# ScalarE applies the instance norm straight from PSUM, and the mask and conv2 convolutions use plain weights for both images at once

## The chip, the cores and the metric

The kernel runs on one core of one Trainium2 chip. The metric is the device time of one execution in microseconds; the median of the timed runs counts. Most executions of a kernel agree within 0.3%, but the three runs of this one before the change spread by 1.4%.

## What is computed

The input x has 8 images of 32 channels and 32x32 pixels, in float32. Two blocks follow each other. The first is a transformer-like block (layer norm over rows, q, k, v by 1x1 and 3x3 convolutions, attention over the channels of a head, a gated convolution block). The change is in the second one:

```python
out = conv2d(x, conv1_w, conv1_b, 1)
mu  = jnp.mean(out, axis=(2, 3), keepdims=True)
var = jnp.var(out, axis=(2, 3), keepdims=True)
out = (out - mu) * jax.lax.rsqrt(var + EPS)
out = jnp.where(out >= 0, out, NEG_SLOPE * out)          # 0.2
# _refine(out)
out1 = conv2d(out, conv2_w, conv2_b, 1)
mask = jax.nn.sigmoid(conv2d(out, mask_w, mask_b, 1))
xm   = out * mask
q, k, v = 1x1 convolutions of xm (k and v of the padded xm)
sims = [jnp.sum(q * k[3x3 neighbour], axis=1) ...]
attn = softmax over the 9 neighbours
out2 = sum of attn * v[neighbour]
result = x + out1 * mask + (1.0 - mask) * out2
```

## The kernel before

The images are worked on in four pairs. A tile of 128 partitions holds four row blocks of 8 rows with 32 channels each, and its free size is 2 images x 256 pixels. A 3x3 convolution reads "planes": for each of the three horizontal shifts 32 partitions that hold the padded image, so that one matmul with 96 rows of weights does a whole row of taps, and three matmuls (dy) accumulate the rest. `sh_ln1`, `sh_ln2`, `sh_x2` and `sh_in` are such planes. They are filled by copies: VectorE writes shift 0 and most of shift 1 (`shift_copies`, L278, seven copies), ScalarE writes the last block of shift 1 and shift 2 (L467, five copies).

The order of each engine's instructions is written out by hand in a function `step` for each engine, and semaphores ("signals") tie the engines together. One step works on three or four pairs at once: the window part of `pair`, the gate part of `pair + 1`, the qk, v and attention part of `pair + 2`, and the first layer norm of `pair + 3`. Pairs 0 and 1 are full steps (step 0 is the body of a loop that runs once, step 1 stands behind it, without the layer norm of pair + 3). Pairs 2 (`but_last`) and 3 (`last`) are written out after them with less work beside them.

The stage that the change touches, in the code of before:

- TensorE: `conv1` (L1112, twelve matmuls of 128x512, in bank 4, or 0 for the last pair), then in the full steps `qk` in three portions (L1132) with the two averages over the four row blocks between them (`average_mean` L1209, `average_var` L1214), then `gram`, `v_by_head` (L1143), `mask_conv` (L1222), `by_head` (L1161), `conv2` (L1222), `window_q` (L1242). In pairs 2 and 3 there is no qk and no v_by_head.
- VectorE: statistics of conv1 in PSUM (`inorm`), mean and second moment (`inorm_mean`), `center` (L880, two ops, subtracts the mean), `variance` (L887, copies the average out of PSUM), `lrelu` (L894), the `sh_in` copies (L278), `head_scores` (L774, L777), `ln2_apply` (L733, L737 and the sh_ln2 copies), `scaled_act` (L906, two ops, times rstd), `head_max` (L782 to L787), `masked` (L912, L916, L922).
- ScalarE: `conv1_evac` (L503, PSUM to `hc`, adds the bias of conv1), two `qk_t_evac` (L479), `in_planes` (L467 into sh_in), `v4_evac` (L484), `ln2_planes` (L467 into sh_ln2), `tanh_mask` (L510).
- GpSimd: `residual`, `rstd` of the layer norms (L376), `inorm_rstd` (L382, variance to the power -1/2, 128x2), `scaled_weights` (L391, two ops: the conv2 and mask weights times rstd of each image), `final` of the pair before (L413, L416).

Leaky ReLU commutes with a positive factor, so the planes hold the centred values only, and rstd is multiplied into the weights, a set for each image. Therefore each convolution is two runs over one image:

```python
for i in range(2):
    for dy in range(3):
        for r in range(R):
            mm = nc.tensor.matmul(ps[C * r:C * r + C, bank, BLK * i:BLK * i + BLK],
                                  w_in[:, i, k, dy, :], ...
```

Each float32 matmul shows as two records in the profile.

Of the kernel before, what the change touches and what calls it, by code (L numbers as in the profile page):

```python
# [66 lines left out]
I_MEAN, I_SHIFT, I_MOMENT, I_WAIT, I_BLOCK_VAR, I_VAR, I_RSTD = range(7)  # L67
# [24 lines left out]
def build(nc, x, shape_consts, vectors, w1_qkv, w3_qkv, w1_gi, w3_gi, conv_w, l1_qkv, r1_t, out):  # L92
    with ExitStack() as ctx:
# [42 lines left out]
        act_c = sb("act_c", [P, 2, BLK])  # L136
        act_in = sb("act_in", [P, 2, BLK])
        w_in = sb("w_in", [P, 2, 2, 3, C])
# [18 lines left out]
        hc = sb("hc", [P, 2, BLK])  # L157
        st6 = sb("st6", [P, 2, 6])
        st = sb("st", [P, 2, 2])
        inorm_v = sb("inorm_v", [P, 7, 2])  # L160
# [93 lines left out]
        def conv1_bank(early):  # L254

            return 0 if early else 4
# [108 lines left out]
        def _(pool):  # L365
# [13 lines left out]
            def inorm_rstd(pair):  # L379

                pool.wait_ge(g_in.sem, g_in.at(pair, 7))
                nc.gpsimd.tensor_tensor(inorm_v[:, I_RSTD, :], inorm_v[:, I_VAR, :], neg_half[:, 0:2], ALU.pow)\  # L382
                  .then_inc(g_inr.sem, 1)

            def scaled_weights(pair):

                pool.wait_ge(g_inr.sem, g_inr.done(pair))
                pool.wait_ge(g_c2.sem, g_c2.before(pair))
                for i in range(2):
                    by_channel = inorm_v[:, I_RSTD, i:i + 1].broadcast_to([P, 2 * 3 * C])  # L390
                    nc.gpsimd.tensor_tensor(w_in[:, i, :, :, :].rearrange("p k y o -> p (k y o)"),  # L391
                                            w_conv[:, 1:3, :, :].rearrange("p k y o -> p (k y o)"),
                                            by_channel, ALU.mult).then_inc(g_win.sem, 1)
# [24 lines left out]
            def step(pair, norm):  # L418
# [5 lines left out]
                scaled_weights(pair + 1)  # L424
# [18 lines left out]
            scaled_weights(0)  # L443
# [6 lines left out]
            scaled_weights(last)  # L450
# [5 lines left out]
        def _(act):  # L456
# [122 lines left out]
            def in_planes(pair):  # L579
                planes("in", act_c, sh_in, g_lr, g_c2, pair)  # L580

            def step(pair, norm):
                load_exp_table()
                squares(1, pair + 1)
                conv1_evac(pair)
                qk_t_evac(pair + 2, 0)
                qk_t_evac(pair + 2, 1)
                in_planes(pair)
# [54 lines left out]
            conv1_evac(but_last)  # L643
# [13 lines left out]
            conv1_evac(last, True)  # L657
# [13 lines left out]
        def _(dve):  # L671
# [201 lines left out]

            def center(pair):

                dve.wait_ge(g_c1_sb.sem, g_c1_sb.done(pair))
                dve.wait_ge(g_in.sem, g_in.at(pair, 5))
                dve.wait_ge(g_lr.sem, g_lr.before(pair))
                for i in range(2):
                    ins = nc.vector.tensor_scalar(hn[:, i, :], hc[:, i, :], inorm_v[:, I_MEAN, i:i + 1], None,  # L880
                                                  ALU.subtract)
                ins.then_inc(g_act.sem, 1)
# [6 lines left out]
            def lrelu(pair):  # L889

                dve.wait_ge(g_c2.sem, g_c2.before(pair))
                dve.wait_ge(g_act.sem, g_act.done(pair))
                planes_read("in", pair)
                nc.vector.scalar_tensor_tensor(out=flat(act_c[:, :, :]), in0=flat(hn[:, :, :]), scalar=SLOPE,  # L894
# [555 lines left out]
```

## Time and profile before

| | us |
|---|---|
| median of three runs | 289.95 |
| lowest and highest run | 288.15 and 292.16 |
| span of the profiled execution, first to last instruction | 286.2 |
| TensorE busy | 222.9 |
| VectorE busy | 189.8 |
| ScalarE busy | 129.2 |
| GpSimd busy | 75.9 |

The profiled execution has no time of its own beside its span; the span leaves out what lies before the first and behind the last instruction. Engines are named in the rows as PE (TensorE), PEld (its weight loads), DVE (VectorE), ACT (ScalarE), POOL (GpSimd). Busy shares are means over the whole span; which engine sets the pace at a place must be read from the timeline there. "The clock" is the granted TensorE clock as a share of full speed (2.4 GHz), so 0.50 is the 1.2 GHz level.

### The profile page before, as it was taken

To read this page: it belongs to the slowest core of one execution; us is meant where nothing else is said; L and a number is where in the kernel's file an instruction comes from. 1 tells how busy PE (TensorE), PEld (TensorE's weight loads), DVE (VectorE), ACT (ScalarE), POOL (GpSimd) and SP (SyncE) were. 2 spreads that over 40 slices of the span, in tenths; PEclk is the share of its full clock that TensorE was granted. 3 is DMA by queue.
4 is the path that set the end of the run, shared out by engine and by line. 5 is a ranking of instruction groups with operands and counts; after the bars stand their busy time and mean duration, and the time that the engine had idled before them with its cause. 6 is when DMAs were issued, how large, how long until landed. Compare 5 with 4: busy or idle time off the path is not lost.

```text
span 286.2 us, 4575 instructions
## 1 busy us (share of the span) xinstructions
PE 222.9 (78%) x1738; PEld 143.5 (50%) x1738; DVE 189.8 (66%) x417; ACT 129.2 (45%) x256; POOL 75.9 (27%) x56
## 2 busy tenths in 40 slices
PE   0429868999669997798999986998529989368963
PEld 0229518824229734654589255745115536136843
DVE  5595365527596768999747974835999738882532
ACT  2230142234383355549822565429347557444440
POOL 3928204004004302540045125000464300304150
PEclk9999997999979999799999997999859999779987
DMA  7210011000011000000000200000000000000101
GB/s 198 53 46 2 0 40 53 0 2 0 1 55 37 2 0 1 2 0 21 0 2 0 73 3 1 2 0 2 0 37 3 0 0 3 0 0 3 39 0 39
DMA packets 3654, 5.17 MB, mean 18 GB/s; under 512 B 1136, under 2 KB 1872, under 8 KB 3632
## 3 DMA queue, kind: packets, MB, share of 16 engines
q1 hardware_dynamic: 3392, 4.29, 5.0%
q10 hardware_dynamic: 240, 0.58, 0.6%
q8 instruction: 14, 0.23, 0.3%
q14 instruction: 8, 0.07, 0.1%
HBM read 3.30 MB, written 1.05 MB: 15 GB/s over the span
## 4 chain that ended last, share of the span: by engine, by line
PE 64%; DVE 17%; ACT 10%; issue 5%; DMA 2%; SPq 0%; ACTq 0%; DVEq 0%
PE ps L1132 16%; PE ps L1186 15%; PE ps L1143 8%; PE ps L1278 6%; PE ps L1302 5%; PE ps L1222 4%; ACT sh_ln L467 4%; ACT p_t L560 3%; DVE sh_in L278 3%; DVE sh_ln L278 2%; DMA w3b<-in_w_gi 2%; PE ps L1262 2%; PE ps L1112 2%; DVE q_bd L933 1%; DVE xm L922 1%
## 5 line engine op out<-in xcount | busy, mean ns | idle before, releaser
L1132 PE MATMUL ps<-w_qk,sh_ln 128*128 128x128 f32 x192 | 46.9, 409 | 11.6 <-DVE sh_ln L278 7.8
L376 POOL TENSOR_TENSOR ln_s<-ln_s,neg_half 128x16 f32<-128x16 f32 x8 | 23.3, 2910 | 112.6 <-DVE ln_s L726 112.6
L1132 PEld LDWEIGHTS ps<-w_qk,sh_ln 128*128 128x128 f32 x192 | 45.6, 330 | 14.3 <-issue 14.3
L1186 PE MATMUL ps<-sh_ln,w_gi 96*128 96x512 f32 x96 | 42.4, 596 | 0.5 <-ACT v L484 0.5
L1222 PE MATMUL ps<-sh_in,w_in 128*32 128x256 f32 x384 | 25.6, 424 | 10.6 <-DVE sh_in L278 10.6
L467 ACT ACTIVATE sh_ln<-ln_out 32x496 f32<-32x496 f32 (+1 forms) x44 | 27.2, 618 | 11.6 <-DVE ln_out L737 11.0
L278 DVE COPY sh_ln<-ln_out 32x496 f32<-32x496 f32 (+2 forms) x60 | 28.0, 466 | 3.4 <-PE ps L1143 2.4
L1186 PEld LDWEIGHTS ps<-sh_ln,w_gi 96*128 96x128 f32 x96 | 17.9, 190 | 22.1 <-issue 21.9
L1222 PEld LDWEIGHTS ps<-sh_in,w_in 128*32 128x32 f32 x384 | 13.3, 123 | 23.3 <-DVE sh_in L278 10.8
L1143 PE MATMUL ps<-sh_ln,w_v 128*32 128x512 f32 x96 | 22.4, 1077 | 0.0
L829 DVE TENSOR_TENSOR gi<-ps,gate 64x512 f32<-64x512 f32 x16 | 11.1, 694 | 13.9 <-ACT gate L498 13.5
L479 ACT ACTIVATE qk_t<-ps 128x512 f32<-128x512 f32 x8 | 4.8, 597 | 34.0 <-PE ps L1132 34.0
L498 ACT ACTIVATE gate<-ps 64x512 f32<-64x512 f32 x16 | 9.4, 587 | 22.1 <-PE ps L1186 22.1
L1302 PE MATMUL ps<-p_t,v_t 128*32 128x64 f32 x256 | 14.2, 235 | 5.5 <-ACT p_t L560 5.5
L1278 PE MATMUL ps<-k_h,q_bd 128*64 128x60 f32 x256 | 17.8, 245 | 0.0
L1278 PEld LDWEIGHTS ps<-k_h,q_bd 128*64 128x64 f32 x256 | 16.6, 158 | 2.0 <-issue 2.0
L278 DVE COPY sh_in<-act_c 32x496 f32<-32x496 f32 (+1 forms) x28 | 17.2, 614 | 0.5
L1302 PEld LDWEIGHTS ps<-p_t,v_t 128*32 128x32 f32 x256 | 13.6, 120 | 7.7 <-issue 7.7
L1112 PE MATMUL ps<-sh_x,w_conv 128*32 128x512 f32 x96 | 12.4, 656 | 3.0 <-DVE sh_x L278 3.0
L467 ACT ACTIVATE sh_in<-act_c 32x496 f32<-32x496 f32 (+1 forms) x20 | 12.3, 617 | 4.9 <-DVE act_c L894 4.7
L400 POOL TENSOR_TENSOR omm<-ones,msk 128x512 f32<-128x512 f32 x4 | 6.6, 1648 | 28.2 <-DVE msk L912 28.0
L467 ACT ACTIVATE sh_x<-x 32x496 f32<-32x496 f32 (+1 forms) x20 | 12.3, 616 | 3.8 <-DVE x L836 3.6
(125 smaller groups left out, 336.5 us busy)
## 6 DMA issues: line engine op xcount, KB each, us to landing
x_norm<-in_x SPq DMA_DIRECT2D x4, 256.0 KB, 2.8
x_res<-in_x SPq DMA_DIRECT2D x4, 256.0 KB, 2.5
out_x<-out_s SPq DMA_DIRECT2D x4, 256.0 KB, 2.0
sh_ln<-ln_out SPq DMA_DIRECT2D x8, 64.0 KB, 2.0
kc<-in_shape_consts ACTq DMA_DIRECT2D x1, 450.0 KB, 5.8
w3b<-in_w_gi SPq DMA_DIRECT2D x1, 288.0 KB, 6.3
vec<-in_vectors SPq DMA_DIRECT2D x1, 131.5 KB, 3.3
w3a<-in_w_qkv ACTq DMA_DIRECT2D x1, 108.0 KB, 3.3
```

Of the source, the lines that this page charges most:

```text
L278: ins = copy(plane(planes)[C * s:C * s + C, :, 1 + RH * r:1 + RH * r + RH, cut_left:cut_left + n], src[C * r:C * r + C, :, :].rearrange("p ...
L376: nc.gpsimd.tensor_tensor(ln_s[n][:, 3, :], ln_s[n][:, 2, :], neg_half[:, :], ALU.pow)\
L467: return nc.scalar.activation(o, i, ACT.Copy)
L498: nc.scalar.activation(gate[EC:P, n, :], ps[0:EC, GI_BANKS[n], :], ACT.Gelu).then_inc(g_gelu.sem, 1)
L829: nc.vector.tensor_tensor(gi[EC * (n % 2):EC * (n % 2) + EC, n // 2, :], ps[EC:P, GI_BANKS[n], :], gate[EC:P, n, :], ALU.mult).then_inc(g_ ...
L1112: mm = nc.tensor.matmul(ps[C * r:C * r + C, bank, :], weight(dy), plane(planes)[:, :, RH * r + dy:RH * r + dy + RH, 0:W], start=(dy == 0), ...
L1132: mm = nc.tensor.matmul(to, sh_ln1[:, i, at:at + D * P - D + 1:D], w_qk[:, dy, :, :, :].rearrange("p d m c -> p (d m c)"), start=(dy == 0) ...
L1143: mm = nc.tensor.matmul(ps[C * d:C * d + C, 2, :], w_v[:, dy, :], xs[:, :, dy:dy + H, d:d + W - D + 1:D], start=(dy == 0), stop=(dy == 2))
L1186: mm = nc.tensor.matmul(ps[:, GI_BANKS[2 * i + h], :], w_gi[:, dy, :, :].rearrange("p m o -> p (m o)"), xs[:, i, y:y + H // 2, 0:W], start ...
L1222: mm = nc.tensor.matmul(ps[C * r:C * r + C, bank, BLK * i:BLK * i + BLK], w_in[:, i, k, dy, :], plane(sh_in)[:, i, RH * r + dy:RH * r + dy ...
L1278: mm = nc.tensor.matmul(ps[C * r:C * r + 2 * C, 5 + bank, KEYS * n:KEYS * n + KEYS], q_bd[:, u, r:r + 2, :].rearrange("p r m -> p (r m)"), ...
L1302: mm = nc.tensor.matmul(o[:, i, a, b:b + 2, :, :], v_t[:, t, C * r:C * r + C], p_t[:, R * t + r, :, :].rearrange("p h m -> p (h m)"), star ...
```

## The change

ScalarE no longer evacuates conv1 with its bias. Once the rstd is known, it applies the whole norm from PSUM, in one activation for each image: scale rstd, bias (bias of conv1 - mean) x rstd. VectorE makes the centre (one small op, L861 in the new numbering), GpSimd multiplies it by rstd (L379) after the power (L376). Lrelu then writes the normalised values, `act_in`, from which the planes are copied and which `masked` reads; `center`, `scaled_act`, `scaled_weights` and the buffers act_c, hc and w_in go. The mask and conv2 convolutions are the same `block_conv` as conv1, over both images, with the weights as loaded.

```diff
             def inorm_rstd(pair):
-                pool.wait_ge(g_in.sem, g_in.at(pair, 7))
+                pool.wait_ge(g_in.sem, g_in.at(pair, 8))
                 nc.gpsimd.tensor_tensor(inorm_v[:, I_RSTD, :], inorm_v[:, I_VAR, :], neg_half[:, 0:2], ALU.pow)\
                   .then_inc(g_inr.sem, 1)
-            def scaled_weights(pair):
...
+                pool.wait_ge(g_inr.sem, g_inr.at(pair, 1))
+                nc.gpsimd.tensor_tensor(inorm_v[:, I_BIAS, :], inorm_v[:, I_CENTER, :], inorm_v[:, I_RSTD, :], ALU.mult)\
+                  .then_inc(g_inr.sem, 1)
...
-            def conv1_evac(pair, early=False):
-                act.wait_ge(g_in.sem, g_in.at(pair, 1))
-                act.wait_ge(g_act.sem, g_act.before(pair))
-                nc.scalar.activation(hc[:, :, :].rearrange("p i m -> p (i m)"), ps[:, conv1_bank(early), :],
-                                     ACT.Identity, bias=vec[:, V_BC1:V_BC1 + 1]).then_inc(g_c1_sb.sem, 1)
+            def inorm_apply(pair, early=False):
+                act.wait_ge(g_inr.sem, g_inr.done(pair))
+                act.wait_ge(g_lr.sem, g_lr.before(pair))
+                for i in range(2):
+                    ins = nc.scalar.activation(hn[:, i, :], ps[:, conv1_bank(early), BLK * i:BLK * i + BLK], ACT.Identity,
+                                               bias=inorm_v[:, I_BIAS, i:i + 1], scale=inorm_v[:, I_RSTD, i:i + 1])
+                ins.then_inc(g_act.sem, 1)
...
+                dve.wait_ge(g.sem, g.at(pair, 5))
+                nc.vector.tensor_scalar(inorm_v[:, I_CENTER, :], inorm_v[:, I_MEAN, :], vec[:, V_BC1:V_BC1 + 1], -1.0,
+                                        ALU.subtract, ALU.mult).then_inc(g.sem, 1)
-            def center(pair):
...
             def lrelu(pair):
...
-                nc.vector.scalar_tensor_tensor(out=flat(act_c[:, :, :]), in0=flat(hn[:, :, :]), scalar=SLOPE,
+                nc.vector.scalar_tensor_tensor(out=flat(act_in[:, :, :]), in0=flat(hn[:, :, :]), scalar=SLOPE,
                                                in1=flat(hn[:, :, :]), op0=ALU.mult, op1=ALU.max)\
                   .then_inc(g_lr.sem, 1)
...
-            def scaled_act(pair):
...
-            def refine_conv(k, bank):
...
             def mask_conv(pair, early=False):
                 planes_ready("in", pair)
-                pe.wait_ge(g_win.sem, g_win.done(pair))
-                refine_conv(1, mask_bank(early)).then_inc(g_mk.sem, 1)
+                block_conv(sh_in, mask_bank(early), lambda dy: w_conv[:, 2, dy, :]).then_inc(g_mk.sem, 1)
 
             def conv2(pair, early=False):
-                refine_conv(0, conv2_bank(early)).then_inc(g_c2.sem, 1)
+                block_conv(sh_in, conv2_bank(early), lambda dy: w_conv[:, 1, dy, :]).then_inc(g_c2.sem, 1)
```

On ScalarE, in a full step, the rows before are these (hc is conv1 in SBUF, qk_t the transposed q and k, sh_in the planes of the activation, v the value tile, sh_ln the ln2 planes, th the tanh):

```order
L464 ACTIVATE ln_q<-ln_c 128x512
L503 ACTIVATE hc<-ps,vec 128x512
L479 ACTIVATE qk_t<-ps 128x512 x2
L467 ACTIVATE sh_in<-act_c 32x2x256
L467 ACTIVATE sh_in<-act_c 32x2x8x31 x4
L484 ACTIVATE v<-ps 128x512
L467 ACTIVATE sh_ln<-ln_out 32x2x256
L467 ACTIVATE sh_ln<-ln_out 32x2x8x31 x4
L510 ACTIVATE th<-ps,half_bm 128x512
```

And now, at the same place:

```order
L448 ACTIVATE ln_q<-ln_c 128x512
L463 ACTIVATE qk_t<-ps 128x512 x2
L489 ACTIVATE hn<-ps,inorm_v 128x256 x2
L451 ACTIVATE sh_in<-act_in 32x2x256
L451 ACTIVATE sh_in<-act_in 32x2x8x31 x4
L468 ACTIVATE v<-ps 128x512
L451 ACTIVATE sh_ln<-ln_out 32x2x256
L451 ACTIVATE sh_ln<-ln_out 32x2x8x31 x4
L497 ACTIVATE th<-ps,half_bm 128x512
```

The reading of conv1 moved from ahead of both qk_t evacuations to behind them, and stands directly ahead of the sh_in copies.

On GpSimd, from the first residual of step 0 to the final ops of pair 0, before (inorm_v holds the small values of the norm, w_in the scaled weights, dif and out_s belong to `final`):

```order
L407 TENSOR_TENSOR res<-res,dif 128x512
L376 TENSOR_TENSOR ln_s<-ln_s,neg_half 128x16 x2
L382 TENSOR_TENSOR inorm_v<-inorm_v,neg_half 128x2
L391 TENSOR_TENSOR w_in<-w_conv,inorm_v 128x192 x2
L413 TENSOR_TENSOR dif<-pv,omm 128x512
L416 TENSOR_TENSOR out_s<-dif,res 128x512
```

And now:

```order
L394 TENSOR_TENSOR res<-res,dif 128x512
L370 TENSOR_TENSOR ln_s<-ln_s,neg_half 128x16 x2
L376 TENSOR_TENSOR inorm_v<-inorm_v,neg_half 128x2
L379 TENSOR_TENSOR inorm_v<-inorm_v 128x2
L400 TENSOR_TENSOR dif<-pv,omm 128x512
L403 TENSOR_TENSOR out_s<-dif,res 128x512
```

The two weight scalings became one small multiply, and the final ops stand directly behind it.

## Rows read from the trace of the kernel before

**Rows 1.** The page: busy time of TensorE, and the last chain by engine.

```profile
PE 222.9 (78%) x1738; PEld 143.5 (50%) x1738; DVE 189.8 (66%) x417; ACT 129.2 (45%) x256; POOL 75.9 (27%) x56
...
PE 64%; DVE 17%; ACT 10%; issue 5%; DMA 2%; SPq 0%; ACTq 0%; DVEq 0%
```

**Rows 2.** Timeline of step 0: start us, length us, engine, line, operation, out<-in, count.

```profile
97.99 3.14 ACT L467 ACTIVATE sh_in<-act_c 32x512 f32<-32x512 f32 x5
...
98.77 0.42 DVE L774 TENSOR_TENSOR sc_m<-ps,kc 128x256 f32<-128x256 f32 x1
...
101.00 2.96 DVE L278 COPY sh_ln<-ln_out 32x512 f32<-32x512 f32 x7
...
104.04 2.80 PE L1222 MATMUL ps<-sh_in,w_in 128*32 128x256 f32 x48
...
104.93 3.13 ACT L467 ACTIVATE sh_ln<-ln_out 32x512 f32<-32x512 f32 x5
...
108.09 0.69 ACT L510 ACTIVATE th<-ps,half_bm 128x512 f32<-128x512 f32 x1
...
113.66 0.98 ACT L532 ACTIVATE k_h<-ps,vec 128x340 f32<-128x340 f32 x2 [0.87 <-PE ps L1251]
```

**Rows 3.** Timeline of step 1: conv1, the sh_in copies, the ln2 planes.

```profile
141.46 2.78 PE L1112 MATMUL ps<-sh_x,w_conv 128*32 128x512 f32 x24
...
154.09 5.40 DVE L278 COPY sh_in<-act_c 32x512 f32<-32x512 f32 x7
...
163.73 3.13 ACT L467 ACTIVATE sh_ln<-ln_out 32x512 f32<-32x512 f32 x5
```

**Rows 4.** Timeline of pair 2, from the power to the mask convolution.

```profile
207.03 1.06 POOL L382 TENSOR_TENSOR inorm_v<-inorm_v,neg_half 128x2 f32<-128x2 f32 x1
...
207.57 5.33 DVE L278 COPY sh_in<-act_c 32x512 f32<-32x512 f32 x7
...
209.39 1.43 POOL L413 TENSOR_TENSOR dif<-pv,omm 128x512 f32<-128x512 f32 x1
210.90 1.31 POOL L416 TENSOR_TENSOR out_s<-dif,res 128x512 f32<-128x512 f32 x1
...
212.96 6.88 PE L1222 MATMUL ps<-sh_in,w_in 128*32 128x256 f32 x96 [6.27 <-DVE sh_in L278]
```

**Rows 5.** Timeline of the last pair, from the power to the mask convolution.

```profile
245.47 1.17 POOL L382 TENSOR_TENSOR inorm_v<-inorm_v,neg_half 128x2 f32<-128x2 f32 x1 [20.93 <-DVE inorm_v L887]
246.10 3.39 DVE L278 COPY sh_in<-act_c 32x512 f32<-32x512 f32 x7
...
249.55 4.77 PE L1222 MATMUL ps<-sh_in,w_in 128*32 128x256 f32 x48 [4.35 <-DVE sh_in L278]
```

**Rows 6.** Groups of instructions: count | busy us, mean ns | idle before, releaser.

```profile
L479 ACT ACTIVATE qk_t<-ps 128x512 f32<-128x512 f32 x8 | 4.8, 597 | 34.0 <-PE ps L1132 34.0
L503 ACT ACTIVATE hc<-ps,vec 128x512 f32<-128x512 f32 x4 | 2.7, 687 | 5.8 <-DVE st L845 5.8
L532 ACT ACTIVATE k_h<-ps,vec 128x340 f32<-128x340 f32 x8 | 3.9, 540 | 1.8 <-PE ps L1251 1.7
L391 POOL TENSOR_TENSOR w_in<-w_conv,inorm_v 128x192 f32<-128x192 f32 x8 | 5.0, 646 | 0.3
L403 POOL TENSOR_TENSOR res<-out,x 128x512 f32<-128x512 f32 x4 | 5.1, 1266 | 17.1 <-ACT out L516 17.0
L906 DVE TENSOR_SCALAR act_in<-act_c,inorm_v 128x256 f32<-128x256 f32 x8 | 2.5, 349 | 0.1
```

**Rows 7.** L715: shortest, median, longest ns; and GpSimd's timeline then.

```profile
L715 DVE SCALAR_TENSOR_TENSOR ln_c<-ln_s,x_norm x4: 691/691/1610, 5.3 to 116.7; 128x512 f32<-128x512 f32 x4
...
116.52 1.28 POOL L405 TENSOR_TENSOR dif<-omm,out 128x512 f32<-128x512 f32 x1
```

**Rows 8.** Windows of pair 2's convolutions: TensorE busy, granted clock, DMA share, GB/s.

```profile
212.96:216.00 3.04, 3.04 (x32) 0.50 0.22 86
216.00:219.84 3.84, 3.84 (x73) 0.99 0.02 4
```

More of the change, by code:

```diff
@@ L63 @@
 V_END = V_OW + D * C
-I_MEAN, I_SHIFT, I_MOMENT, I_WAIT, I_BLOCK_VAR, I_VAR, I_RSTD = range(7)
+I_MEAN, I_SHIFT, I_MOMENT, I_WAIT, I_BLOCK_VAR, I_VAR, I_RSTD, I_CENTER, I_BIAS = range(9)
 class Signal:
@@ L423, in step @@
                 inorm_rstd(pair + 1)
-                scaled_weights(pair + 1)
                 final(pair)
@@ L449, in _ @@
             inorm_rstd(last)
-            scaled_weights(last)
             final(but_last)
@@ L579, in in_planes @@
             def in_planes(pair):
-                planes("in", act_c, sh_in, g_lr, g_c2, pair)
+                planes("in", act_in, sh_in, g_lr, g_c2, pair)
             def step(pair, norm):
@@ L584, in step @@
                 squares(1, pair + 1)
-                conv1_evac(pair)
                 qk_t_evac(pair + 2, 0)
                 qk_t_evac(pair + 2, 1)
+                inorm_apply(pair)
                 in_planes(pair)
@@ L656, in _ @@
             window_exp(but_last)
-            conv1_evac(last, True)
+            inorm_apply(last, True)
             in_planes(last)
@@ L892, in lrelu @@
                 dve.wait_ge(g_act.sem, g_act.done(pair))
+                dve.wait_ge(g_xm.sem, g_xm.before(pair))
                 planes_read("in", pair)
-                nc.vector.scalar_tensor_tensor(out=flat(act_c[:, :, :]), in0=flat(hn[:, :, :]), scalar=SLOPE,
+                nc.vector.scalar_tensor_tensor(out=flat(act_in[:, :, :]), in0=flat(hn[:, :, :]), scalar=SLOPE,
                                                in1=flat(hn[:, :, :]), op0=ALU.mult, op1=ALU.max)\
@@ L898, in in_planes @@
             def in_planes(pair):
-                planes("in", act_c, sh_in, g_lr, g_c2, pair)
-            def scaled_act(pair):
-                dve.wait_ge(g_inr.sem, g_inr.done(pair))
-                dve.wait_ge(g_lr.sem, g_lr.done(pair))
-                dve.wait_ge(g_xm.sem, g_xm.before(pair))
-                for i in range(2):
-                    ins = nc.vector.tensor_scalar(act_in[:, i, :], act_c[:, i, :], inorm_v[:, I_RSTD, i:i + 1], None,
-                                                  ALU.mult)
-                ins.then_inc(g_sc.sem, 1)
+                planes("in", act_in, sh_in, g_lr, g_c2, pair)
             def masked(pair):
@@ L913, in masked @@
                 dve.wait_ge(g_xm.sem, g_xm.at(pair, 1))
-                dve.wait_ge(g_sc.sem, g_sc.done(pair))
+                dve.wait_ge(g_lr.sem, g_lr.done(pair))
                 dve.wait_ge(g_v.sem, g_v.before(pair))
@@ L991, in step @@
                 inorm_mean(pair)
-                center(pair)
                 variance(pair)
@@ L997, in step @@
                 ln2_apply(pair + 1)
-                scaled_act(pair)
                 head_max(pair + 2)
@@ L1071, in _ @@
             inorm_mean(last, True)
-            center(last)
             variance(last, True)
@@ L1077, in _ @@
             window_probs(but_last)
-            scaled_act(last)
             masked(last)
```

41 lines of the change are left out of this document (5 added, 36 removed).

## The prediction

> **What bounds the kernel now.** I read the page's shares first, then its chain, then the timeline around each instance norm. TensorE is busy for 222.9 of 286.2 us and the chain puts 64% on it, 17% on VectorE, 10% on ScalarE [rows 1]. No engine is simply full: the end is set by a relay, and what counts is where each of the four instance norms stands in it. They stand in two kinds of place.
>
> Pairs 0 and 1 (the two full steps). While the norm is worked out, TensorE has other work: the qk and v convolutions of pair+2. In step 0, ScalarE comes from the second qk_t evacuation to the sh_in copies at 97.99, waits for the v convolution, evacuates it, copies the ln2 planes (L467, 104.93 to 108.06), and only then does tanh (L510, 108.09) release mask, xm and the window work. The mask convolution had begun at 104.04 and was over by 106.84, so tanh waited for ScalarE's own queue [rows 2]. Step 1 repeats this: its ln2 planes run from 163.73 to 166.86 [rows 3].
>
> Pair 2 and the last pair. TensorE has nothing else to do there. It stands until the shifted planes of the normalised activation are written: pair 2's mask convolution starts at 212.96, right behind VectorE's seven sh_in copies (207.57 plus 5.33) [rows 4]; the last pair's starts at 249.55, behind copies that ended at 249.49 [rows 5]. Whatever makes these planes later is paid in full.
>
> **What the change removes.** VectorE loses two centering ops and two scaling ops a pair (the scaling ones 349 ns each, and the centering ones, of the same shape, taken for as much), 1.4 us; GpSimd loses two weight scalings of 646 ns, 1.3 us [rows 6]. On TensorE 48 short matmuls a convolution pair become 24 long ones over the same columns. The trace has both kinds at full clock: 2.80 us for one convolution in 48 records of 256 columns [rows 2], 2.78 us for conv1, in 24 records of 512 [rows 3]. So I put this at nothing. Before, the planes were made from the centred values, which need only the mean; the variance, the power -1/2 and the scaled weights were made beside them. Now all of it stands ahead of the planes.
>
> **What it adds to the path.** Power, then a GpSimd multiply of 128x2, then two ScalarE activations of 128x256, then lrelu, then the copies. Lrelu (0.69) and the copies were there already.
>
> The multiply: GpSimd took 646 ns for 192 columns and 1266 ns for 512 [rows 6], a slope of 1.94 ns a column, which leaves 0.27 us at two columns. Bounds: nothing, and what the power on 128x2 takes, 1.17 at most [rows 4, 5]. I take 0.27, and 0.08 for the handover: L413 ends at 210.82 and L416, which waits for it, starts at 210.90 [rows 4].
>
> The two activations: the shape with a per-partition bias took 687 ns at 512 columns and 540 at 340, so 468 at 256; without a bias 512 columns took 597 [rows 6], so one per-partition operand costs 0.09, and the new scale operand as much again: 0.56 each. Two of this kind in a row overlap by 0.1 (the k_h pair took 0.98 for 2 x 0.54 [rows 2, 6]), so 1.02. Bounds: 0.84 (no cost for the scale) and 1.37 (two of the 512 form).
> The Trainium skill ("ScalarE: Activation LUTs", What ACT_TABLE_LOAD costs) gives each [128,1] pointer operand about 93 ns and says neighbouring activations overlap by as much; by its formula, an estimate, the two would take 1.08. The 90 ns between the two rows agrees, and no row here shows a scale operand by pointer.
>
> Pairs 0 and 1. Power and multiply are hidden: they wait for the second average, which TensorE gives before the last half of qk, and ScalarE must evacuate that half first. The new order puts the activations behind both qk_t evacuations, so hn stands at 97.99 + 1.02 = 99.01, lrelu ends at 99.74, VectorE's seven copies (2.96, as for the ln2 planes) end at 102.72, ScalarE's (3.14) at 102.9. The mask convolution starts at 104.04: still hidden, by 1.1 us. But queued behind the copies on VectorE are head_scores and ln2_apply. They took 2.23 from L774 at 98.77 to the first ln2 copy at 101.00; now they start at 102.74 and ln2_out is ready at 104.97. ScalarE wants it at 104.93 [rows 2]. So all the slack is used up to within 0.05 us; I charge 0.05 to each of the two steps, 0.1 together. Behind that, VectorE's ln2 copies end at 107.93 and the three small head_max ops at 108.6, ahead of tanh's end at 108.83; the removed scaling ops are what makes this fit. From here every 0.1 us that hn is later costs 0.1 in each of these steps.
>
> Pair 2. Power ends at 208.09, multiply at 208.44, hn at 208.5 + 1.02 = 209.52. Directly behind the multiply GpSimd starts the two final ops of pair 1, which stood at 209.39 and 210.90 [rows 4]. One runs 208.5 to 209.77 (1.27, the plain length of such an op). A copy of VectorE beside such an op waits for its end: seven copies took 5.33 here where the same seven took 2.96 elsewhere [rows 2, 4]. A scalar_tensor_tensor on 128x512 (L715, started at 116.7, while L405 ran) took 1610 ns where its fellows took 691 [rows 7]; lrelu is such an instruction, and 0.69 is what I take for it undisturbed. So lrelu runs 209.8 to 210.5, GpSimd's second op waits for it and ends near 211.8, the first copy ends at 212.1 and six more of 0.42 at 214.6. TensorE starts at 214.65, not 212.96: 1.7. If lrelu were free of GpSimd it would be 1.1.
> The Trainium skill ("SBUF — State Buffer", SBUF: two separate sides) calls this an exclusive lock on a shared port pair, taken also by a VectorE op with two SBUF inputs against a GpSimd op that reads SBUF; by it pair 2 comes out at the 1.7, without it at 1.1. The 1610 ns row agrees.
>
> Last pair. GpSimd has no final op there. Power ends at 245.47 + 1.17 = 246.64, multiply at 246.99, hn at 248.07, lrelu at 248.80, ScalarE's five copies (3.14) at 251.97. TensorE starts at 252.0 for 249.55: 2.45. VectorE's probabilities and v_t of pair 2 are queued behind its sh_in copies and slip by 2.3; they are ready before this mask convolution ends, as before.
>
> **Sum.** 0.1 + 1.7 + 2.45 = 4.25 us. The profiled execution has a span of 286.2 and would have 290.5. The profile gives no time for what lies around it; the median of the runs, 289.95, is 3.75 above the span and the fastest run, 288.15, 1.95. Counted from the median: 294.2 us, 1.5% slower. About 2% (5.8 us) is what a measurement of this kernel can tell from no change.
> With all low bounds (activations -0.18 and multiply -0.27 in pair 2 and in the last, lrelu -0.6, the full steps -0.1): 2.65, so 292.6. With the high ones: 297.4, worked out below.
>
> **Rivals.**
> Slower, by the floor price of small instructions. If a short activation costs the full 0.687 (+0.35 for two) and the small multiply as much as the power (+0.9), the two full steps tip over their edge by 0.35 each and the other two pairs pay 1.25 each: 4.25 + 0.7 + 2.5 = 7.45, 297.4 us. It decides for slower from 1.55 us above my sum. For it: the power on 128x2 takes over 1 us. Against it: 540 ns at 340 columns, and 646 ns for GpSimd's 192.
> Slower, by the clock. In pair 2 the granted clock was 0.50 (the 1.2 GHz level) while TensorE stood, stayed 0.50 for the first 3.04 us of the convolutions, then 0.99 [rows 8]. The change lengthens both standstills. If the clock stayed low through both convolutions of pair 2, they would take 4 x 2.80 = 11.2 for 6.88, and the last mask convolution 5.6 for 4.77: 5.1 more, 299.3. Against it: after the 6.27 us of standstill in pair 2 the clock was back within the first half of the convolutions; the last pair stood for less, 4.35, and its convolution was still slow throughout, so the length of the standstill doesn't decide it alone.
> No loss, by the clock. If TensorE were back at full speed sooner at both places, the convolutions would take 5.6 and 2.8: 3.3 us less, 290.9.
> Faster, by the work removed. VectorE's eight centering and eight scaling ops sum to 5.6 us, and the held-up copies of pairs 1 and 2 (5.40 and 5.33 for 2.96) give 4.8 more [rows 2, 3, 4]. All on the path it would be 10.4 us, 279.6. For it: VectorE is 17% of the chain. Against it: in steps 0 and 1 tanh waits for ScalarE, and the copies end over 1 us before TensorE asks for them even in the new order; in the other pairs what takes their place is longer.
>
> **How the numbers follow.** Forecast 0.58, its own range 292.6 to 296. Floor prices 0.18, low clock 0.07, early clock 0.12, faster 0.05. Faster by over 2%: 0.05. Slower: 0.18 + 0.07 and 0.04 for the forecast's own upper end, 0.29. Within 2%: 0.66. The range leaves out the fast case and the low clock, 0.12, and some at the edges: 290.5 to 298.0.
>
> **What would show it.** In the profile after: two activations on hn of about 0.56; a GpSimd multiply of 0.2 to 0.4; in both full steps ScalarE's ln2 planes right behind the v evacuation, in step 1 sh_in copies of 2.96 instead of 5.40; in both, tanh 10.1 us behind the end of the qk_t evacuation, as now (108.09 less 97.97); TensorE's idle time before the mask convolution at 6.27 + 1.7 in pair 2 and 4.35 + 2.45 in the last. Wrong it would be if tanh in the full steps moved by over 0.3, if the multiply took over 0.6, or if the low-clock stretches behind the standstills changed by over 1 us together.

## The result and the profile after

Over 21 runs of each kernel the median went from 289.82 to 293.01 us; the ratio of the changed kernel to the old one is 1.0116, with a 95% interval of 1.0087 to 1.0144. That is 3.4 us (2.5 to 4.2) slower, against 4.25 us in the prediction, whose range and sign held. One execution of each kernel is far off and is left out of the ratio: 494.62 us of the old one, and 1032.66 us of the changed one, which was the one profiled first, with TensorE at about a fifth of its speed throughout. Without these two the means differ by 2.8 us. The profile shown here is that of the run "again" of the same kernel, whose span is 290.9 us.

The page of the changed kernel, for comparison with [rows 1] (busy us, share of the span, instructions):

```profile
span 290.9 us, 4170 instructions
...
PE 225.1 (77%) x1546; PEld 137.8 (47%) x1546; DVE 180.7 (62%) x405; ACT 130.3 (45%) x260; POOL 69.9 (24%) x52
```

VectorE lost 9.1 us of work (189.8 before), GpSimd 6.0, TensorE 192 matmul records, and the kernel got slower: a busy share that falls says nothing while the relay is what sets the end.

The timeline of step 0 on ScalarE answers to [rows 2] (start, length, engine, line, operation; in brackets the idle time before and its releaser):

```profile
97.45 0.60 ACT L463 ACTIVATE qk_t<-ps 128x512 f32<-128x512 f32 x1 [5.47 <-PE ps L1098]
97.94 1.01 ACT L489 ACTIVATE hn<-ps,inorm_v 128x256 f32<-128x256 f32 x2
99.78 3.14 ACT L451 ACTIVATE sh_in<-act_in 32x512 f32<-32x512 f32 x5 [0.82 <-DVE act_in L875]
104.39 0.60 ACT L468 ACTIVATE v<-ps 128x512 f32<-128x512 f32 x1 [1.48 <-PE ps L1109]
105.01 3.13 ACT L451 ACTIVATE sh_ln<-ln_out 32x512 f32<-32x512 f32 x5
108.17 0.69 ACT L497 ACTIVATE th<-ps,half_bm 128x512 f32<-128x512 f32 x1
```

All of this trace lies 0.08 us later than the old one from before step 0 on, so the tanh at 108.17 (108.09 before) and the ln2 planes at 105.01 (104.93) have not moved at all. ScalarE writes its planes of the activation 1.8 us later than before (VectorE its own 4.5 us later), but v's evacuation still waits 1.48 us for TensorE behind them.

Pair 2, on GpSimd, ScalarE, VectorE and TensorE, for comparison with [rows 4]:

```profile
208.09 0.70 POOL L376 TENSOR_TENSOR inorm_v<-inorm_v,neg_half 128x2 f32<-128x2 f32 x1
208.87 0.19 POOL L379 TENSOR_TENSOR inorm_v<-inorm_v 128x2 f32<-128x2 f32 x1
209.01 1.26 POOL L400 TENSOR_TENSOR dif<-pv,omm 128x512 f32<-128x512 f32 x1
209.09 1.02 ACT L489 ACTIVATE hn<-ps,inorm_v 128x256 f32<-128x256 f32 x2 [4.89 <-POOL inorm_v L379]
210.21 0.69 DVE L875 SCALAR_TENSOR_TENSOR act_in<-hn 128x512 f32<-128x512 f32 x1 [2.27 <-ACT hn L489]
210.35 1.67 POOL L403 TENSOR_TENSOR out_s<-dif,res 128x512 f32<-128x512 f32 x1
...
210.94 3.91 DVE L272 COPY sh_in<-act_in 32x512 f32<-32x512 f32 x7
...
214.90 1.94 PE L1078 MATMUL ps<-sh_in,w_conv 128*32 128x512 f32 x8 [7.16 <-DVE sh_in L272]
```

The new relay can be read off: power, multiply, hn, lrelu, copies, one behind the other. TensorE stands for 7.16 us, 6.27 before. In the last pair, for comparison with [rows 5]:

```profile
249.71 1.02 ACT L489 ACTIVATE hn<-ps,inorm_v 128x256 f32<-128x256 f32 x2 [4.59 <-POOL inorm_v L379]
...
254.82 4.42 PE L1078 MATMUL ps<-sh_in,w_conv 128*32 128x512 f32 x24 [6.40 <-ACT sh_in L451]
```

Here it stands for 6.40 us against 4.35. So the change adds 0.89 + 2.05 = 2.94 us of standstill, which accounts for the measured 3.4 us to within the interval. The two profiled spans differ by more, 4.7 us. The rest is TensorE's clock, which differs from run to run (experiments below keep it at full speed): the scores of step 0 ran more at low clock (0.9 us), pair 2's two convolutions took 8.18 us for 6.88, the last mask convolution 4.42 for 4.77, and the stretch from the start of the last window output to the end took 0.2 us less.

### The profile page after: what moved, and what is told of

Its sections match the earlier page's. It is cut to its first block, busy times and chain, and to the rows that moved or that the text cites. A ratio compares the mean times of both kernels' runs of the same rounds, so it can differ in the third digit from the quotient of the medians.

```text
span 1030.8 us, 4170 instructions
## 1 busy us (share of the span) xinstructions
PE 988.5 (96%) x1546; PEld 508.8 (49%) x1546; DVE 174.5 (17%) x405; ACT 130.6 (13%) x260; POOL 69.5 (7%) x52
## 4 chain that ended last, share of the span: by engine, by line
PE 96%; DVE 2%; ACT 1%; issue 1%; DMA 1%; POOL 0%; SPq 0%; ACTq 0%; DVEq 0%; POOLq 0%
PE ps L1152 25%; PE ps L1078 18%; PE ps L1098 13%; PE ps L1232 7%; PE ps L1256 6%; PE ps L1109 6%; PE ps L1216 4%; PE ps L1205 3%; PE ps L1134 2%; PE ps L1196 2%; PE ps L1243 2%; PE ps L1121 2%; PE ps L1160 2%; PE ps L1226 1%; DMA w3b<-in_w_gi 1%
## 5 line engine op out<-in xcount | busy, mean ns | idle before, releaser
L1152 PE MATMUL ps<-sh_ln,w_gi 96*128 96x512 f32 x96 | 256.2, 3004 | 0.5 <-issue 0.5
L1152 PEld LDWEIGHTS ps<-sh_ln,w_gi 96*128 96x128 f32 x96 | 82.6, 876 | 160.3 <-issue 160.3
L1078 PE MATMUL ps<-sh_in,w_conv 128*32 128x512 f32 x192 | 128.0, 2947 | 13.5 <-DVE sh_in L272 7.1
L1098 PEld LDWEIGHTS ps<-w_qk,sh_ln 128*128 128x128 f32 x192 | 128.3, 916 | 16.2 <-issue 16.2
L1098 PE MATMUL ps<-w_qk,sh_ln 128*128 128x128 f32 x192 | 131.9, 1064 | 2.7 <-DVE sh_ln L272 2.7
L1232 PEld LDWEIGHTS ps<-k_h,q_bd 128*64 128x64 f32 x256 | 71.1, 594 | 8.9 <-issue 8.9
L1232 PE MATMUL ps<-k_h,q_bd 128*64 128x60 f32 x256 | 73.4, 642 | 0.0
L1256 PE MATMUL ps<-p_t,v_t 128*32 128x64 f32 x256 | 64.8, 686 | 2.8 <-ACT p_t L547 2.8
L1078 PE MATMUL ps<-sh_x,w_conv 128*32 128x512 f32 x96 | 63.8, 2914 | 0.0
L1216 PE MATMUL ps<-w_bd,xw 128*60 128x128 f32 x128 | 47.2, 1037 | 0.0
L451 ACT ACTIVATE sh_ln<-ln_out 32x496 f32<-32x496 f32 (+1 forms) x44 | 27.2, 617 | 12.7 <-DVE ln_out L724 12.1
L272 DVE COPY sh_ln<-ln_out 32x496 f32<-32x496 f32 (+2 forms) x60 | 25.4, 423 | 13.7 <-PE ps L1109 12.8
```

The costliest lines, as they stand in the source:

```text
L272: ins = copy(plane(planes)[C * s:C * s + C, :, 1 + RH * r:1 + RH * r + RH, cut_left:cut_left + n], src[C * r:C * r + C, :, :].rearrange("p ...
L451: return nc.scalar.activation(o, i, ACT.Copy)
L1078: mm = nc.tensor.matmul(ps[C * r:C * r + C, bank, :], weight(dy), plane(planes)[:, :, RH * r + dy:RH * r + dy + RH, 0:W], start=(dy == 0), ...
L1098: mm = nc.tensor.matmul(to, sh_ln1[:, i, at:at + D * P - D + 1:D], w_qk[:, dy, :, :, :].rearrange("p d m c -> p (d m c)"), start=(dy == 0) ...
L1152: mm = nc.tensor.matmul(ps[:, GI_BANKS[2 * i + h], :], w_gi[:, dy, :, :].rearrange("p m o -> p (m o)"), xs[:, i, y:y + H // 2, 0:W], start ...
L1216: mm = nc.tensor.matmul(ps[KSLOT * half:KSLOT * half + KEYS, (7, 4)[t // 4], P * (t % 4):P * (t % 4) + P], xw[:, u, :], w_bd[:, 2, :], sta ...
```

## The experiments

Ratios are to the old kernel, run on the same chip in the same session, with 95% intervals.

### The changed kernel again

No edit.

> The changed kernel as it is. The comparison gave a ratio of 1.0116 (1.0087 to 1.0144), so 3.4 us; the forecast's sum was 4.25, of it 1.7 in pair 2, 2.45 in the last pair and 0.05 in each full step. The sum's theory: in the profile, tanh in the full steps 10.1 to 10.2 us behind the end of the second qk_t evacuation, TensorE idle about 8.0 us before pair 2's mask convolution (6.27 before) and 6.8 before the last one's (4.35 before), two hn activations in 1.02, the GpSimd multiply 0.27. Rival (the clock gave something back): the idle times grow as forecast, but the convolutions behind them take less than 6.88 and 4.77.

Ratio 1.0097 (1.0063 to 1.0132). The standstills were 7.16 and 6.40 us. 8.0 and 6.8 had been forecast, so both waits had been overestimated, by 0.8 and 0.4. The groups of instructions show the terms (count, then busy us and mean ns, then idle time before):

```profile
L489 ACT ACTIVATE hn<-ps,inorm_v 128x256 f32<-128x256 f32 x8 | 4.1, 561 | 9.5 <-POOL inorm_v L379 9.5
L376 POOL TENSOR_TENSOR inorm_v<-inorm_v,neg_half 128x2 f32<-128x2 f32 x4 | 2.8, 700 | 29.2 <-DVE inorm_v L867 29.2
L379 POOL TENSOR_TENSOR inorm_v<-inorm_v 128x2 f32<-128x2 f32 x4 | 0.8, 194 | 0.3
```

The two activations were 561 ns each and 1.02 us together, as worked out from the old rows. The estimate by the formula of the Trainium skill ("ScalarE: Activation LUTs", What ACT_TABLE_LOAD costs) had been 1.08. The multiply took 194 ns, not 270. And the power took 700 ns in all four places, where it had been 1.06 to 1.17 us [rows 4, 5]. In the old kernel VectorE's lrelu (L894) ran beside it, in the new one lrelu waits for it. These are the old kernel's lrelu in pair 2 and in the last pair, and then lrelu and power in pair 2 of the old kernel with idle matmuls (below), where the power began later within lrelu:

```profile
206.85 0.69 DVE L894 SCALAR_TENSOR_TENSOR act_c<-hn 128x512 f32<-128x512 f32 x1
245.38 0.69 DVE L894 SCALAR_TENSOR_TENSOR act_c<-hn 128x512 f32<-128x512 f32 x1
...
207.81 0.69 DVE L894 SCALAR_TENSOR_TENSOR act_c<-hn 128x512 f32<-128x512 f32 x1
208.17 0.89 POOL L382 TENSOR_TENSOR inorm_v<-inorm_v,neg_half 128x2 f32<-128x2 f32 x1
```

Each time the power ends 0.55 to 0.57 us behind the end of lrelu (208.09 behind 207.54, 246.64 behind 246.07, 209.06 behind 208.50), whenever it began: its row holds the rest of lrelu. The copies that run beside its second half add nothing that can be seen. No run moved lrelu by itself.

### The final ops of pair 1 later

GpSimd holds the two final ops of pair 1 until the sh_in planes of pair 2 are copied.

```diff
                 inorm_rstd(pair + 1)
+                if not norm:
+                    pool.wait_ge(planes_by["in"]["dve"].sem, planes_by["in"]["dve"].done(pair + 1))
                 final(pair)
```

> The changed kernel, with GpSimd's two final ops of pair 1 held until VectorE has copied the sh_in planes of pair 2. If lrelu and the first copy of pair 2 were held up by those two ops, lrelu follows hn at once, the seven copies take 2.96, and TensorE starts pair 2's mask convolution about 1.4 us sooner than in the changed kernel: ratio to before about 1.007. If GpSimd doesn't hold VectorE up, no stage moves and the ratio stays 1.012.

Ratio 1.0126 (1.0061 to 1.0191): 1.007 had been forecast, and no gain can be seen. But in the timeline the copies took 2.96 us instead of 3.91:

```profile
210.47 0.69 DVE L877 SCALAR_TENSOR_TENSOR act_in<-hn 128x512 f32<-128x512 f32 x1 [2.47 <-ACT hn L491]
211.19 3.12 ACT L453 ACTIVATE sh_in<-act_in 32x512 f32<-32x512 f32 x5 [0.82 <-DVE act_in L877]
211.19 2.96 DVE L272 COPY sh_in<-act_in 32x512 f32<-32x512 f32 x7
...
214.46 1.93 PE L1080 MATMUL ps<-sh_in,w_conv 128*32 128x512 f32 x8 [6.66 <-ACT sh_in L453]
```

So GpSimd did hold VectorE up, by 0.95 us in the first copy. Lrelu itself had not been held: it started 0.10 us behind the end of hn in both. And of the 0.95 only 0.5 reached TensorE (7.16 to 6.66), since ScalarE's five copies, 3.12 us long, now end last.

### Without the multiply

```diff
-                pool.wait_ge(g_inr.sem, g_inr.at(pair, 1))
-                nc.gpsimd.tensor_tensor(inorm_v[:, I_BIAS, :], inorm_v[:, I_CENTER, :], inorm_v[:, I_RSTD, :], ALU.mult)\
-                  .then_inc(g_inr.sem, 1)
...
-                                               bias=inorm_v[:, I_BIAS, i:i + 1], scale=inorm_v[:, I_RSTD, i:i + 1])
+                                               bias=inorm_v[:, I_CENTER, i:i + 1], scale=inorm_v[:, I_RSTD, i:i + 1])
```

> The changed kernel without GpSimd's multiply; the bias of the hn activations is the centre not yet multiplied by rstd, so the values of the norm differ. The sum's theory: each of pair 2 and the last pair starts its mask convolution 0.35 us sooner (0.27 and the handover 0.08), the full steps don't move; about 0.7 us in all. The rival of floor prices (multiply 1.17): 1.25 sooner in each, 2.5 us in all.

This kernel leaves out the multiply, so its bias is the centre alone. The standstills went from 7.16 to 6.99 us and from 6.40 to 6.13, so the multiply is worth 0.17 and 0.27 us, where 0.35 each had been forecast. The ratio, 1.0116 (1.0078 to 1.0154), can't show 0.4 us. The rival of floor prices falls: neither the multiply nor the activations cost what it took for them.

### One image at a time, with plain weights

```diff
+            def split_conv(planes, bank, weight):
+                for i in range(2):
+                    for dy in range(3):
+                        for r in range(R):
+                            mm = nc.tensor.matmul(ps[C * r:C * r + C, bank, BLK * i:BLK * i + BLK], weight(dy),
...
-                block_conv(sh_in, mask_bank(early), lambda dy: w_conv[:, 2, dy, :]).then_inc(g_mk.sem, 1)
+                split_conv(sh_in, mask_bank(early), lambda dy: w_conv[:, 2, dy, :]).then_inc(g_mk.sem, 1)
```

(conv2 likewise.)

> The changed kernel, but mask and conv2 convolutions run one image after the other again, in 24 matmuls of 256 columns each instead of 12 of 512, still with plain weights. The sum's theory: no difference (2.80 against 2.78 us a convolution at full clock). A rival that counts instructions: 4 to 5 us slower in all, if the weight loads' 23 us of idle before them were a cost.

Ratio 1.010 (1.0055 to 1.0145), against 1.0097 with the long matmuls. The profile of the run has the same standstills to the hundredth (7.16 and 6.40) and 2.80 us a convolution in the full steps, where the long ones take 2.78. So the long matmuls, the part of the change that the unscaled weights made possible, are worth 0.02 us a convolution. The other kernel loads weights twice as often and stands no longer for it: the 23 us of idle time in the row of PEld were no cost.

### The edge in the full steps

An idle ScalarE activation of 128x512 ahead of hn, in the full steps only.

```diff
                 qk_t_evac(pair + 2, 1)
+                nc.scalar.activation(idle[:, :], ones[:, :], ACT.Copy)
                 inorm_apply(pair)
```

> The changed kernel with one idle ScalarE copy of 128x512 (about 0.6 us, writes a buffer that nobody reads) ahead of the hn activations in the two full steps only. The edge theory (no slack is left there): tanh moves by 0.5 to 0.6 in both full steps, 1.1 to 1.2 us slower in all than the changed kernel. Rival (the full steps have hidden slack, since TensorE has other work): no change.

Ratio 1.0147 (1.0114 to 1.0181), 0.9 us above the changed kernel's 1.0116 and 1.4 above its 1.0097, with four executions and intervals of about 1 us either way; the ratio alone would not show it. The rows of step 0 show the relay that the prediction described, moved as a whole:

```profile
98.67 1.01 ACT L490 ACTIVATE hn<-ps,inorm_v 128x256 f32<-128x256 f32 x2
...
103.50 0.42 DVE L763 TENSOR_TENSOR sc_m<-ps,kc 128x256 f32<-128x256 f32 x1
...
105.01 0.69 DVE L726 TENSOR_TENSOR ln_out<-vec,ln_d 128x512 f32<-128x512 f32 x1
105.73 2.96 DVE L273 COPY sh_ln<-ln_out 32x512 f32<-32x512 f32 x7
```

The second hn ends at 99.68, ln2_out at 105.70. In the changed kernel tanh came 4.05 us behind the start of the mask convolution, in step 0 (108.17 less 104.12), and in the old one 4.05 as well; here it comes 4.55 behind it (108.89 less 104.34). So 0.5 of the added 0.52 us (hn starts 1.01 us behind the start of the second qk_t evacuation instead of 0.49) reach tanh, and in step 1 the same 0.5. The full steps have no slack left, while TensorE's own work still covers the mask convolution.

### The old kernel with the final ops later, or earlier

The late version has the edit above, in the old kernel. The early one moves `final(pair)` ahead of `rstd(1, pair + 2)` in both full steps.

> The kernel of before with GpSimd's two final ops of pair 1 held until VectorE has copied the sh_in planes of pair 2. If they cost the 5.33 us copies of pair 2 their extra time: copies in about 3.4 (the scaled weights still run beside them), the mask convolution of pair 2 1.9 us sooner, the kernel 1.5 to 2 us faster than before: 0.993 to 0.995. If the copies are long for another reason: 1.000.

> The kernel of before with GpSimd's final ops of a pair ahead of the layer norm's power of the same step, in both full steps (right behind the window output of that pair). The sh_in copies of step 1 and pair 2 are freed as in the late variant, but the ops now run beside ln2_center; its scalar_tensor_tensor with two SBUF inputs would wait about 1 us. In pair 2 the statistics of conv1 are queued behind it, so of the 1.9 us gained about 1 is given back: 0.996 to 0.998. If GpSimd holds nothing up: 1.000.

Late: ratio 0.9979 (0.9949 to 1.0009), 0.993 to 0.995 forecast. Pair 2's standstill fell from 6.27 to 4.33 us, the 1.9 us of the forecast, and the time hardly moved. Early: 1.0014 (0.9971 to 1.0057), 0.996 to 0.998 forecast; the same 4.33 us, but from the start of conv1 to the mask convolution 11.76 us, where it was 12.72 in the old kernel and 10.77 in the late version. Of the 1 us that is given back, 0.8 is in ln2_center (its L715 took 1.47 us for 0.69). In both, the waits did what they should, and the gain went elsewhere. The late version's timeline shows one candidate:

```profile
211.24 7.63 PE L1224 MATMUL ps<-sh_in,w_in 128*32 128x256 f32 x96 [4.33 <-DVE sh_in L278]
...
248.58 5.14 PE L1224 MATMUL ps<-sh_in,w_in 128*32 128x256 f32 x48 [4.36 <-DVE sh_in L278]
256.99 4.63 PE L1304 MATMUL ps<-p_t,v_t 128*32 128x64 f32 x64 [2.24 <-ACT p_t L562]
```

These three took 6.88, 4.77 and 3.15 us in the old kernel. The same instructions, 2.6 us longer in this execution, at low clock. Behind the standstills of pair 2 and of the last pair TensorE starts at the 1.2 GHz level in all eight profiles so far (that of the 1032.66 us left out): the two convolutions of pair 2 took 6.77 to 8.23 us and the last mask convolution 4.42 to 5.35, where 5.4 and 2.8 are their times at full clock. Whether low clock is what ate the gain was open here; the old kernel with both edits (below) speaks against it. This called for experiments in which TensorE doesn't stand.

### Idle matmuls in the standstills of pair 2 and the last pair

```diff
+            def keep_busy(n, early=False):
+                for _ in range(n):
+                    nc.tensor.matmul(ps[:, mask_bank(early), :], kc[:, K_ID:K_ID + P], ones[:, :], start=True, stop=True)
...
             conv1(but_last)
+            keep_busy(2)
             average_mean(but_last)
             average_var(but_last)
+            keep_busy(7)
...
             average_var(last, True)
+            keep_busy(6, True)
```

(In the old kernel 6 and 4 instead of 7 and 6; with the late final ops 4 and 4.) Their results are overwritten by the mask convolution.

> The changed kernel with idle TensorE matmuls (128x512, identity against ones, into the bank that the mask convolution overwrites) in the standstills of pair 2 (2 ahead of the averages, 7 behind) and of the last pair (6). Clock theory: the granted clock stays at full speed, pair 2's two convolutions take 5.6 us instead of 6.8 to 8.2, the last mask convolution 2.8 instead of 4.4 to 5.4, the window output after it 3.15: 3.5 to 5.5 us faster than the changed kernel, ratio to before 0.993 to 1.000. Rival (the clock doesn't follow TensorE's activity, or TensorE's first matmuls behind a wait are slow for another reason): no convolution gets shorter, and the kernel is 0 to 1 us slower than the changed one.

> The kernel of before with the same idle matmuls (2 and 6 in pair 2, 4 in the last pair). Clock theory: 6.88 becomes 5.6 and 4.77 becomes 2.8, and perhaps 4.70 at the end 3.15: 3 to 4.5 us faster than before, ratio 0.985 to 0.990. The difference to the changed kernel with idle matmuls is then the pure wait that the change added, 3.2 us (0.13 in each full step, 0.9 in pair 2, 2.05 in the last pair). Rival (part of the change's cost is clock): the difference is clearly smaller than 3.2.

> The kernel of before with the late final ops and the idle matmuls (2 and 4, 4). Alone, the late ops shortened pair 2's standstill from 6.27 to 4.33 us, but the convolutions behind it took 7.63 for 6.88 and the time hardly moved (0.998). If the clock ate it, the 1.9 us show here: ratio 0.978 to 0.984. Rival (the slack lies elsewhere): the same as with the idle matmuls alone.

The changed kernel: 1.0022 (0.9987 to 1.0058), just above its forecast. The old one: 0.989 (0.9852 to 0.9928), as forecast. The old one with late final ops: 0.9882 (0.983 to 0.9934), where 0.978 to 0.984 had been forecast. Windows over the old kernel without idle matmuls, over its standstill in pair 2, both convolutions, the last mask convolution and the last window output (TensorE busy, granted clock, DMA share, GB/s):

```profile
206.50:212.90 6.40, 0.19 (x1) 0.50 0.00 0
212.96:219.84 6.88, 6.88 (x97) 0.78 0.11 40
249.55:254.30 4.75, 4.75 (x49) 0.58 0.00 0
277.20:281.90 4.70, 4.70 (x64) 0.64 0.01 3
```

and with them (6 and 4), over the first three of these places and the window output that follows the last mask convolution:

```profile
207.50:213.90 6.40, 5.38 (x14) 1.00 0.00 0
213.95:219.35 5.40, 5.40 (x97) 1.00 0.14 52
249.30:252.10 2.80, 2.80 (x48) 1.00 0.00 0
255.70:260.40 4.70, 4.68 (x65) 0.64 0.02 3
```

The clock theory held for the places that were filled (6.88 to 5.40, 4.77 to 2.80) and failed for the one behind: that window output had been at full clock in the old profile (3.15) and was now at 0.64. It has a standstill of its own in front, 1.39 us here and 2.24 in the old profile. The difference between the new and the old kernel with idle matmuls is 0.0132, 3.8 us with an interval of some 1.5 either way, which doesn't part 3 from 4.

The Trainium skill ("TensorE: Matmul & The Clock Gate", HAM oscillation — how this bites in real kernels) says that waits between bursts of matmuls put the array back to the low clock; the 0.50 of the standstill and the 1.00 of the filled one agree. The Trainium skill's figure of less than 1% of a typical kernel ("TensorE: Matmul & The Clock Gate", Part 1: The HAM clock gate) is for the ramp at the start, which no run here prices. What is lost behind the standstills of this kernel is more, as the runs of the next section show.

The late final ops bring nothing on top: 285.76 us is the median with and without them. So their 1.9 us do not show with the convolutions at full clock either, which speaks for the rival (the slack lies elsewhere). The ratio's interval just reaches the forecast, but the traces decide it. The rows of pair 2, with idle matmuls alone and then with the late final ops too:

```profile
214.65 0.69 DVE L737 TENSOR_TENSOR ln_out<-vec,ln_d 128x512 f32<-128x512 f32 x1
215.38 2.96 DVE L278 COPY sh_ln<-ln_out 32x512 f32<-32x512 f32 x7
225.73 1.38 PE L1255 MATMUL ps<-xm,w_bd 128*128 128x340 f32 x4
...
212.73 1.65 DVE L739 TENSOR_TENSOR ln_out<-vec,ln_d 128x512 f32<-128x512 f32 x1
214.41 3.96 DVE L278 COPY sh_ln<-ln_out 32x512 f32<-32x512 f32 x7
218.43 5.42 PE L1188 MATMUL ps<-sh_ln,w_gi 96*128 96x512 f32 x12 [1.01 <-DVE sh_ln L278]
225.38 1.38 PE L1257 MATMUL ps<-xm,w_bd 128*128 128x340 f32 x4 [0.51 <-issue]
```

The mask convolution starts 1.92 us sooner (212.03 for 213.95). But the final ops now run beside ln2_apply and the ln2 copies and hold these up, TensorE waits 1.01 us for them and 0.51 more ahead of the key convolution, and that one starts only 0.35 us sooner. The hold-up was moved, not removed.

### Idle matmuls at every standstill, in the old and the new kernel

The same, with the late final ops, and also in the full steps between window_q and window_k (1) and ahead of window_scores (2), ahead of the last scores (1), and ahead of both late window outputs (2 each).

```diff
                 window_q(pair)
+                keep_busy(1, bank=0)
                 window_k(pair)
+                keep_busy(2, bank=0)
                 window_scores(pair)
...
             probs_transposed(last)
+            keep_busy(2, bank=2)
             window_out(last)
```

> As before this one, and idle matmuls also ahead of the key convolution and of the window scores of the full steps (1 and 2), ahead of the last scores (1) and ahead of both window outputs at the end (2 each). Clock theory: the first half of the scores in the full steps takes 1.8 instead of 2.7 to 3.3 us, the last window output 3.15 instead of 4.7: 2 to 4 us more than without, ratio 0.967 to 0.976. Rival: the idle matmuls push back the work that follows them, and it is no faster than without, or slower.

Ratio 0.9732 (0.9696 to 0.9767), as forecast: 281.01 us, the fastest version, 2.7% below the old kernel. The seven runs lie within 1.6 us, six of them within 0.4, where those of the old kernel spread over 4 to 5. Windows over its standstill in pair 2, the convolutions, the last mask convolution, the window output after it and the scores of step 0:

```profile
205.50:210.00 4.50, 3.74 (x10) 1.00 0.00 0
210.06:215.50 5.44, 5.38 (x96) 1.00 0.14 51
247.00:249.80 2.80, 2.80 (x48) 1.00 0.02 6
253.68:256.80 3.12, 3.12 (x66) 1.00 0.00 0
116.10:120.00 3.90, 3.88 (x62) 1.00 0.00 0
```

> The changed kernel with the late final ops and idle matmuls at all the places of the fastest version of the old one (6 behind the averages in pair 2 and 6 in the last pair, where the old one has 4 and 4). With the clock at full speed in both, only the waits differ: the standstills of pair 2 were 6.66 against 4.33 us (both with late final ops), those of the last pair 6.40 against 4.35, and tanh comes 0.13 later in each full step: 2.33 + 2.05 + 0.26 = 4.6 us more than the old one's 281.0, so 285.6, ratio to before 0.989. Rival (what the waits cost is partly covered when the clock is steady): 2 us or less more, 283 or below. Rival (the waits cost more than their length, through the clock): over 6 us more.

Ratio 0.9851 (0.98 to 0.9901), 284.3 us, its six runs within 0.7. That is 3.3 us above the old one's 281.01. The two were timed on different chips; by their ratios the difference is 0.0119, 3.4 us with an interval of 1.8 either way. 4.6 had been forecast. The traces say it more closely. By the two traces, from the start of one stage to the start of the next: the two full steps 0.0, apart from the window output of step 0, which ran at low clock in the profiled execution of the old version (4.70 us for 3.15; this execution took 282.41 us where the others took about 281.0). (The 0.13 a step that I had put down was a wrong reading: I had counted from the first sh_in copy of the old kernel and the first hn activation of the new one, and hn begins before the evacuation ahead of it has ended.) Pair 2 from conv1 to the mask convolution 12.91 for 10.61, so 2.3 more, and then 0.8 less up to the key convolution; the last pair 12.41 for 10.37, 2.0 more, then 0.27 less up to the window output. 2.3 - 0.8 + 2.0 - 0.3 is 3.2. In all other stages the two traces agree to within 0.05 us, but for the output transfer at the very end, 0.2 shorter in the new one. The 0.8 is the one place where the removed work pays. These are the old kernel's rows in pair 2:

```profile
216.44 0.61 DVE L908 TENSOR_SCALAR act_in<-act_c,inorm_v 128x256 f32<-128x256 f32 x2
...
216.97 0.42 DVE L914 TENSOR_SCALAR msk<-th 128x512 f32<-128x512 f32 x1
...
223.43 1.38 PE L1257 MATMUL ps<-xm,w_bd 128*128 128x340 f32 x4 [0.52 <-issue]
```

With the late final ops VectorE is the slow one there: the ln2 planes end at 216.4, the scaling stands ahead of the mask, and TensorE waits for the planes (1.02 us before its gate convolution) and again before the key convolution (0.52). In the new kernel the mask follows the planes at once, at 216.91 although the mask convolution had begun 0.76 later, and the second wait is gone.

## Why the prediction came out as it did

- The sign and the mechanism were right: the norm became a serial relay ahead of the planes, and it costs where TensorE has no other work. The size was somewhat too high: 4.25 us forecast, 3.4 measured (2.5 to 4.2).
- Full steps, 0.1 forecast: 0.0 measured. That they stand on an edge was right; "The edge in the full steps" showed it.
- Pair 2, 1.7 forecast: 0.89 measured, the term that was most off. Three parts of it were mis-sized. The power was taken from the old rows (1.06), which hold the rest of an lrelu that ran beside it; alone it takes 0.70. The prediction used this very hold-up for lrelu and the copies, but not for the power. The multiply was 0.19 for 0.27. And the hold-up by the final ops was reckoned at 1.4 us, 0.2 for lrelu and 1.2 for the first copy; the copy lost 0.95 (1.36 us for 0.41) and lrelu nothing: the first final op began 0.08 us ahead of hn, not with it, and only its last 0.06 us fell beside lrelu.
- Last pair, 2.45 forecast: 2.05 measured; again the power (0.71 for 1.17) and the multiply (0.19 for 0.27), less 0.1 for handovers that were longer than reckoned.
- Convolutions with plain weights on both images, nothing forecast: nothing measured (1.010 against 1.0097 with and without).
- The two activations, 1.02 forecast: 1.01 to 1.02.
- The rivals. Floor prices: refuted by the rows; the power's 1.06 to 1.17 us, which had spoken for it, were 0.70 and a wait. Faster by the work removed: refuted where the kernel stands; removed VectorE work pays 0.8 us only in a version in which VectorE has become late. The clock: neither rival came true, the added waits account for the cost within the interval. But the clock is by far the largest thing that the runs found: nearly all of the 8 us between the old kernel (289.07 in that session) and the fastest version, since the late final ops brought about 0.4 by the traces and nothing by the medians.
- What stays open: whether the change by itself makes TensorE run at low clock a little more often. 2.94 us of waits against 3.4 (2.5 to 4.2) leaves room for it and doesn't ask for it. The prediction had named a change of over 1 us in the low-clock stretches as a sign of being wrong, and between the two profiles shown it is 0.95. Single profiles don't settle it: the convolutions behind both standstills took 12.1 to 12.7 us together in the five profiles of the changed kernel and its variants, and 11.7 to 12.8 in the three of the old one.

## What to carry to other kernels

Fewer instructions and less busy time are worth nothing until the relay that sets the end is shorter; before a factor is moved from the weights into the data, ask whether the step that now waits for it had been running beside it. Price a small op from rows where nothing runs beside it, if nothing will run beside it in the new place. Where TensorE must stand, fill the standstill with matmuls whose result nobody reads: it was worth 2.7% here together with the late final ops, and it makes small differences measurable, since the spread between executions fell from 5 us to 1.6 and less. And before an op is moved out of the way of one wait, look at what it will run beside in its new place: the late final ops took 1.9 us out of one standstill and put most of it into the next.

## What the runs showed of the hardware that was not expected

- GpSimd's power on 128x2 takes 0.70 us alone, and 0.89 to 1.17 us where VectorE's lrelu, which reads two SBUF inputs, ran beside its start; it then ended 0.55 to 0.57 us behind lrelu. A multiply of the same shape takes 0.19.
- Behind standstills of 1.4 to 2.4 us the next stretch ran at a granted clock of 0.57 to 0.64 in some profiles (0.64 in the window output after the last mask convolution of the old kernel with idle matmuls, 0.57 in the scores of step 0 of the changed kernel) and at full clock in others: that window output, behind 2.24 us, took 3.15 us in four of the eight profiles without idle matmuls, and 4.63 to 4.73 in the other four.
- A GpSimd op on 128x512 held a VectorE copy or two-input op beside it up by 0.8 to 1.0 us, wherever it was put: the first sh_in copy of pair 2 (1.36 us for 0.41), ln2_center (1.47 for 0.69), ln2_apply and the ln2 copies (1.65 for 0.69, 3.96 for 2.96). So 1.9 us less in one wait brought 0.6 us (0.9979, an interval that includes nothing), and nothing with idle matmuls in both.
